# Attention: the subtraction that makes the low halves of k, on GpSimd in place of VectorE

## The reference, cut to what matters

```python
q_lat = q @ q2l_w.T + q2l_b
k_lat = k @ kv2l_w.T + kv2l_b
q_lat = q_lat * cos + _rotate_half(q_lat) * sin
k_lat = k_lat * cos + _rotate_half(k_lat) * sin
q_for_k = q_lat @ wqk_w.T + wqk_b
att = jnp.einsum('bhql,bhkl->bhqk', q_for_k, k_lat) * L ** (-0.5)
att = jnp.where(causal[None, None], att, -jnp.inf)
att = jax.nn.softmax(att, axis=-1)
```

## Time and profile before

| | us |
|---|---|
| median of 3 runs | 2293.83 (2292.97 to 2294.26) |
| profiled execution | 2283.68, span 2281.5 |
| attention, units in their rhythm | about 100 to 1440 of the span |
| experts and the end | about 1530 to the end of the span |

### The profile page before, as it was taken

One profiled execution on the slowest core, in us unless ns is written; L12 is line 12 of the kernel. 1 busy time (PEld: TensorE's weight loads), 2 busy tenths in 40 slices (PEclk: granted clock), 3 DMA queues, 4 the chain that ended last, 5 costly groups with the idle time before them and its releaser, 6 DMA issues. The chain is left out here.

```text
span 2281.5 us, 43376 instructions
## 1 busy us (share of the span) xinstructions
PE 2026.2 (89%) x12076; PEld 1409.2 (62%) x12076; DVE 1730.7 (76%) x4972; ACT 1374.5 (60%) x3259; POOL 1414.6 (62%) x1662
## 2 busy tenths in 40 slices
PE   3899999999999999999998999973399999999785
PEld 2555655655655655655655565522299999999664
DVE  3677688788778778778768868816488888888498
ACT  1266656656655655665665665643188888888465
POOL 2364565676666675585477467344477777777476
PEclk7799999999999999999999999975699999999898
DMA  6565557556646655666555655315022222222483
GB/s 184 130 140 146 121 123 171 124 115 150 152 99 136 164 127 118 155 136 136 155 117 126 157 121 114 89 36 211 20 73 76 74 75 75 76 74 76 184 307 133
DMA packets 165829, 284.84 MB, mean 125 GB/s; under 512 B 54072, under 2 KB 78288, under 8 KB 165456
## 3 DMA queue, kind: packets, MB, share of 16 engines
q1 hardware_dynamic: 144032, 236.77, 43.0%
q0 software_dynamic: 17152, 35.87, 5.2%
q10 hardware_dynamic: 4416, 9.44, 1.1%
HBM read 100.37 MB, written 38.23 MB: 61 GB/s over the span
## 5 line engine op out<-in xcount | busy, mean ns | idle before, releaser
L566 ACT ACTIVATE probs<-scores_T 128x512 f32<-128x512 f32 (+3 forms) x1536 | 659.9, 494 | 307.5 <-PE scores_T L455 295.0
L814 POOL TENSOR_SCALAR_AFFINE_SELECT probs<-probs 128x256 f32<-128x256 f32 x512 | 215.1, 429 | 530.6 <-ACT probs L566 528.8
L721 DVE TENSOR_REDUCE neg_part<-ring 128x1 f32<-128x512 f32 x512 | 334.1, 686 | 147.4 <-PE ring L514 145.8
L514 PE MATMUL ring<-k_stack,q_stack_b 96*128 96x512 f32 (+3 forms) x1024 | 398.3, 413 | 17.2 <-DVE neg_max L726 14.6
L455 PE MATMUL scores_T<-q_stack_b,k_stack 98*128 98x512 f32 (+3 forms) x1024 | 355.6, 393 | 4.2 <-ACT probs L566 2.9
L472 PE MATMUL o_ps<-probs,v_ones 128*17 128x512 f32 (+3 forms) x3072 | 333.0, 507 | 12.3 <-POOL probs L814 12.3
L726 DVE CUSTOM_DVE_ANT_0 ring<-ring,mask 128x384 f32<-128x384 f32 (+3 forms) x512 | 241.8, 510 | 95.5 <-PE ring L514 89.9
L514 PEld LDWEIGHTS ring<-k_stack,q_stack_b 96*128 96x128 f32 x1024 | 197.2, 194 | 156.9 <-DVE neg_max L726 52.0
L726 DVE CUSTOM_DVE_ANT_0 ring<-ring,mask,neg_part 128x384 f32<-128x384 f32 (+3 forms) x512 | 258.9, 553 | 25.8 <-PE ring L514 23.4
L455 PEld LDWEIGHTS scores_T<-q_stack_b,k_stack 98*128 98x128 f32 x1024 | 193.1, 195 | 116.5 <-ACT probs L566 93.4
L1131 ACT ACTIVATE o_sb<-ht_ps,ln_b,ln_g 128x128 f32<-128x128 f32 x544 | 217.7, 450 | 75.5 <-PE ht_ps L1080 72.4
(11 more groups left out here) (194 smaller groups left out, 4693.1 us busy)
## 6 DMA issues: line engine op xcount, KB each, us to landing
u_rot<-u SPq DMA_DIRECT2D x128, 256.0 KB
k_stack<-u_rot SPq DMA_DIRECT2D x128, 256.0 KB
lat_w<-lat_split SPq DMA_DIRECT2D x32, 512.0 KB
q_stack_a<-u_rot SPq DMA_DIRECT2D x64, 256.0 KB
q_stack_b<-u_rot SPq DMA_DIRECT2D x64, 256.0 KB
k_stack<-u SPq DMA_DIRECT2D x64, 256.0 KB
y<-y_rows SPq DMA_DIRECT2D x32, 512.0 KB, 5.3
x_raw<-in_xT SPq DMA_DIRECT2D x16, 512.0 KB, 5.8
```

Of the source, the lines that this page charges most:

```text
L514: nc.tensor.matmul(out[:, 0:k1 - k0], q_stack[qb // 4][0:3 * L, row_buf(n, qb // 4), h, P * (qb % 4):P * (qb % 4) + P], k_stack[0:3 * L, n ...
L566: nc.scalar.activation(probs[:, s % 2, h, cols], sc[t % 3][:, HALF - w:HALF], ACT.Exp).then_inc(exp_done, 1)
L721: nc.vector.tensor_reduce(neg_part[:, n % 2, part_col], src[:], AX_X, ALU.max, negate=True).then_inc(max_taken, 1)
L814: nc.gpsimd.affine_select(both, both, [[0, 2], [1, P]], ALU.is_ge, zero, base=0, channel_multiplier=-1).then_inc(kept, 1)
```

## The change

KL goes from VectorE's list to GpSimd's. The instruction is the same subtraction of 128x512 with the same waits and the same signal; 64 of them run, two for each unit. Its place on the axis stays −33.375 with a pace of 2.125, and GpSimd has no lag for it (VectorE's was −0.375).

```diff
                 elif kind == "QL":
...
-                elif kind == "KL":
-                    part = it[2]
-                    cols = slice(HALF * part, HALF * part + HALF)
-                    dve.wait_ge(k_hi_ready, 2 * n + part + 1)
-                    nc.vector.tensor_tensor(u[1][:, cols].bitcast(F32R), u[1][:, cols], hi[1][:, cols],
-                                            ALU.subtract).then_inc(k_lo_ready, 1)
                 elif kind == "S":
...
+                elif kind == "KL":
+                    part = it[2]
+                    cols = slice(HALF * part, HALF * part + HALF)
+                    pool.wait_ge(k_hi_ready, 2 * n + part + 1)
+                    nc.gpsimd.tensor_tensor(u[1][:, cols].bitcast(F32R), u[1][:, cols], hi[1][:, cols],
+                                            ALU.subtract).then_inc(k_lo_ready, 1)
                 elif kind == "Y":
```

## The result

The changed kernel is faster: a median of 2285.03 us (20 runs) against 2293.39 us (20 runs), ratio 0.997 with a 95% interval of 0.9958 to 0.9982. Run again with the experiments it gave 0.9966 (0.9948 to 0.9985). That is 7 to 8 us less, where 17 us more were forecast; 2285 us lies under the low end of the range.

The account below looks back on a forecast made before the run. TensorE was taken as the bound, so what counts is how long it stands still. Terms +16.8 + 10.2 + 2.1 − 9.8 − 2 = +17.3 us on 2283.68, plus 10.15 to the median, gave 2311.1; range 2290 to 2328.

Parts of the forecast that it names:

- the range: Whole kernel: 2290 to 2328 us, to leave out no more than 2 in 10; bounds of the terms 2298 to 2325.
- Where TensorE stands still: TensorE in the attention: KL can touch two waits, for VectorE's maxima (15.2 us) and the stack of k (7.1 us).
- KL's price and place on GpSimd: GpSimd's list: KL costs 1.29 us in place of 0.69 and, in kind 1, ends 2.7 us later.
- kind 1: Units 5, 9, ... 29: k's stack, already late, comes 2.4 us later in seven units, +16.8 us (9 to 18).
- Does the landing move as far?: Stack of k in kind 1: of KL's 2.7 us delay, 2.4 was taken to reach the landing, near the full shift.
- Rival 2: Not slower, chance 0.22: kind 1's stack lands by the traffic, not the issue; shift under about 0.5 us, −8, 2286.
- The clock behind the waits: TensorE after kind 1's longer stalls: clock falls to 0.50, 6 × 1.7 = +10.2 us (0 to 20).
- Kind 2: Units 6, 10, ... 30: KL no longer holds up VectorE's maxima; TensorE's 1.17 us wait goes, 1.4 each, −9.8 us.
- Kind 0 and the rest: Units 4, 8, ... 28, and 1: stack 0.7 us later, +2.1 (0 to 5); other waits for maxima −2 (−5 to 0).
- rival 3: More than forecast, chance 0.15: KL on GpSimd holds up VectorE's instructions with two SBUF inputs, as x_lo; +9, 2320.
- The end of the sum: Whole kernel: profiled 2283.68 us with +17.3 gives 2301.0; the median's 10.15 above the profile was kept, giving 2311.1.
- kind 3: Units with n % 4 = 3: GpSimd is idle for 6.91 us before the select, KL comes sooner, S(0,0,0) did not wait.

Follow-up runs that it names:

- small_q: Kernel before, but in units with n % 4 = 1 (from unit 5) the q stack's part 1 DMAs copy 8 source rows, not 128; ratio 0.9937.

## Why the prediction was wrong, point by point

- *Where TensorE stands still*: right. KL's effect came through the two waits that were named, and moving kinds 0 and 3 alone could not be told from no change.
- *KL's price and place on GpSimd*: right. 1.28 us in the median, and in unit 25 an issue 2.6 us later, against 2.7 (1.4 to 2.6 in the seven units of kind 1).
- *Does the landing move as far?* This is the step that failed, and with it the term of +16.8. I took 2.4 us of 2.7, "since nothing in these rows says what held them", though 8.36 us against at most 7.02 in another unit was in front of me. Measured from the first S block of the unit before, the landing moved by 0.4 us on the mean of the seven units (−0.1 to 1.1), and by 0.3 us in the second profiles. What held it was the q stack's backlog, which small_q took away. TensorE's wait grew by more than the landing moved, 0.9 us on the mean (−0.1 to 1.4), because TensorE came to it 0.5 us sooner (in unit 25, 0.2 of it is there with kinds 0 and 3 moved alone too, and 0.2 with kind 1 alone). That part costs nothing, as the prediction had it for what was in VectorE's way. So the units of kind 1 took 2.5 us more in all (1.8 us in the second profiles), where 16.8 were forecast.
- *Rival 2* had the mechanism ("the traffic and not the issue") and the size: a shift under 0.5 us and a time of 2286, against 0.4 us and 2285 measured. Its time is so near partly by luck: kind 1 cost more than its 5 us, with the clock, and kind 2 gained more than its 9.8.
- *The clock behind the waits*: right in kind, too large. Waits of 1.6 to 1.7 us lost it in units 9 and 13 of the profile after and kept it in units 17 and 29. The stretches at half clock that began between 180 and 1460 us were 47.6 and 64.6 us in two profiles of before, 61.2 and 68.0 in two of after: on the mean 8.5 us more, a loss of 4 us, not 10.2. The two profiles of one kernel differ by as much, so this is a rough figure. After unit 25's wait:

```profile
1178.30:1181.70 3.40, 3.40 (x12) 2.82 (x12) 0.81 (x4) 0.62 (x2) 0.00 (x0) 0.51 0.03 7
```

- *Kind 2*: the right mechanism, undersized. 1.4 us a unit was taken for the wait of 1.17 and the restart. The score block behind C that had waited comes 1.5 us sooner (units 18, 30), and the blocks behind it win another 0.2 to 0.3, which the prediction left out. A unit without a loss of the clock takes 43.9 us in place of 45.6: 12 us for seven, against 9.8, and above the bound of 11.
- *Kind 0 and the rest*: 41.2 us in place of 41.5 in most units of kind 0 of the profile after, a gain of 0.3 and no cost of 0.7, but for units 1, 4 and 8, where the stack came later and TensorE waited. The other waits for the maxima, for which −2 was taken, went from 7.0 to 7.7 us, and in the second profiles from 8.1 to 6.6.
- *The ports* (rival 3): small but real. x_lo went from 1273 to 1398 ns on the mean. In one place TensorE waited more: among the last score blocks of unit 6, while k of unit 7 was rotated, it stood 3.86 us for the maxima, in place of 1.26 before. The rows of before, then those of after:

```profile
346.03 0.69 DVE L694 CAST x_hi<-x_raw 128x1024 fp32r<-128x1024 f32 x1 [1.04 <-DMA x_raw<-in_xT]
346.76 1.22 DVE L696 TENSOR_TENSOR x_lo<-x_raw,x_hi 128x1024 fp32r<-128x1024 f32 x1
348.36 0.39 PE L514 MATMUL ring<-k_stack,q_stack_b 96*128 96x256 f32 x1 [1.26 <-DVE neg_max L726]
```

```profile
346.69 1.69 DVE L694 CAST x_hi<-x_raw 128x1024 fp32r<-128x1024 f32 x1 [1.62 <-DMA x_raw<-in_xT]
347.80 1.71 POOL L814 TENSOR_TENSOR u<-u,u_rot 128x512 fp32r<-128x512 f32 x1
348.42 2.17 DVE L696 TENSOR_TENSOR x_lo<-x_raw,x_hi 128x1024 fp32r<-128x1024 f32 x1
350.97 0.58 PE L514 MATMUL ring<-k_stack,q_stack_b 96*128 96x256 f32 x1 [3.86 <-DVE neg_max L720]
```

  KL's part of this is the 0.9 us by which it held x_lo; x_lo takes 2.2 to 2.3 us there in all six profiles with unit 7's KL on GpSimd in the changed kernel's order, and 1.2 us in the six with it on VectorE and in the two with the lag of −1.5. The rest is not shown to be KL's: VectorE waited longer for the DMA of x and its cast took 1.0 us longer, and with unit 7's KL on VectorE the same wait was anything from none to 2.82 us.
- *The range*: 2298 to 2325 was called the bounds of the terms, but they add up to 2287 and 2334.
- *The end of the sum*: 10.15 us were added for the distance from profile to median. For after it is 0.7 us. An absolute forecast carries the luck of the profile that it starts from.

What the kinds took in all, after less before, in the two pairs of profiles (us; each with its losses of the clock):

```
                        first pair   second pair
up to S of unit 4          +4.6         +2.6
kind 0, from unit 8        -1.7         +0.7
kind 1                     +2.5         +1.8
kind 2                     -8.9         -8.1
kind 3                     +1.5         -0.3
behind S of unit 31        +3.0         -0.9
whole span                 +1.1         -4.2
```

The forecast of the same was +17.3, and the runs say −7 to −8. What parts the pairs from the runs is of the size of the spread of single profiles and is not settled; nor is why the start came later by more than the wait of unit 1 (1.5 us).

## What to carry to other kernels

Before a DMA's start is moved, look at when the DMAs issued before it land. Where they are still under way well after its issue (here 3.7 us and more), its landing is not its issue plus a constant, and a delay up to the end of that backlog is cheap, while one beyond it costs in full. A longer wait on an engine is not yet a later end: take the time from one fixed point to the next, since the engine may only have come to the wait sooner. When an instruction's mean is far above its median, find the few places that make the mean, and move the instruction only there: a quarter of this change made all of its gain that can be told, and another quarter paid for it.

## What the runs showed of the hardware that was not expected

- The stack's three DMAs of 256 KB took 5.3 us from first issue to last landing at the least, in every kind, and 6.8 to 8.2 us when an earlier stack landed 3.7 to 5.4 us behind their issue. The whole DMA share in the 2.4 us after such an issue was 0.67 (unit 25 of before), so not all engines were busy all of the time. Which were is not shown.
- The same wait of 1.7 us on TensorE lost the clock in some units and not in others of one execution, for 3.4 us or 6.8 us. In one profile of the kernel with kind 2 alone a loss lasted 17 us and made the unit 54.2 us long instead of 49.
- VectorE's KL, held for 4.26 us, was not let in between GpSimd's Y and its add, which followed each other without a gap. The Trainium skill ("SBUF — State Buffer", Who interferes with whom) has the lock held to the instruction's end; the rows add that a back-to-back GpSimd instruction kept it.
